# Cross attention: keys of two steps in one 512-column product

## The reference, cut to what matters

```python
q = (query @ Wq + bq).reshape(B, L, NKV, G, HDIM)        # 32 x 64 x 8 x 4 x 128
k_, v_ = jnp.split(kv @ Wkv + bkv, 2, axis=-1)           # 8 heads of keys and values
scores = jnp.einsum('blkgd,bmkd->bkglm', q, k) * scale   # 64 x 64 per batch and head
attn = jax.nn.softmax(scores, axis=-1)
o = jnp.einsum('bkglm,bmkd->blkgd', attn, v).reshape(B, L, NHEAD * HDIM)
return o @ Wo + bo
```

## Time and profile before

| | |
|---|---|
| median of three runs | 2743.34 us |
| profiled execution | 2743.87 us |
| its span | 2742.1 us |
| TensorE matmul busy | 2684.1 us, 98% |
| VectorE busy | 2022.1 us, 74% |
| GpSimd busy | 1621.1 us, 59% |
| ScalarE busy | 1537.9 us, 56% |
| granted clock of TensorE, mean | 0.994 |
| cross attention, first score matmul of step 0 | at 1642.16 us |

### The profile page before, as it was taken

How to read it: one execution, slowest core, us unless ns; L and a number is a source line. 1 busy time by engine, 2 the same in 40 slices (tenths; PEclk the granted TensorE clock), 3 DMA queues, 4 the chain that set the end, 5 groups by cost and what they waited for, 6 DMA issues and landing times.

```text
span 2742.1 us, 64050 instructions
## 1 busy us (share of the span) xinstructions
PE 2684.1 (98%) x26496; PEld 2374.8 (87%) x26496; DVE 2022.1 (74%) x4005; ACT 1537.9 (56%) x3207; POOL 1621.1 (59%) x1379
## 2 busy tenths in 40 slices
PE   7999999999999999999999999999999999999997
PEld 6889888889899999999998988888888888888876
DVE  6676667667677777667777668887778878777887
ACT  5566566656666665666665645554445455444445
POOL 6887887788777666676666763232324433333235
PEclk9999999999999999999999999999999999999998
DMA  6233223323325313322331331111112111111111
GB/s 177 77 93 99 86 80 103 94 70 104 107 61 168 92 48 88 84 72 72 84 87 52 83 98 43 35 54 39 45 41 59 51 43 40 50 35 43 32 32 62
DMA packets 91483, 197.70 MB, mean 72 GB/s; under 512 B 20664, under 2 KB 21304, under 8 KB 89144
## 3 DMA queue, kind: packets, MB, share of 16 engines
q1 hardware_dynamic: 71480, 154.80, 20.2%
q10 hardware_dynamic: 17664, 34.61, 3.8%
q0 software_dynamic: 2048, 4.20, 0.5%
HBM read 176.78 MB, written 16.78 MB: 71 GB/s over the span
## 4 chain that ended last, share of the span: by engine, by line
PE 84%; POOL 7%; DVE 5%; issue 2%; ACT 1%; DMA 0%; DVEq 0%; ACTq 0%
PE bank L1865 29%; PE big L1865 28%; PE bank L1957 14%; PE big L1937 12%; POOL ptl L799 3%; POOL gathered L774 2%; PE big L1957 2%; POOL wqTl L534 1%; ACT pth L981 0%; DVE xol L1514 0%; DVE P L1690 0%; POOL wkvTl L534 0%; PE big L1858 0%; POOL oTl L804 0%; DVE nmx L1417 0%
## 5 line engine op out<-in xcount | busy, mean ns | idle before, releaser
L799 POOL TENSOR_TENSOR ptl<-P,pth 128x576 fp32r<-128x576 f32 x512 | 727.5, 1438 | 291.1 <-ACT pth L981 290.6
L972 ACT ACTIVATE P<-big,nmx 128x576 f32<-128x576 f32 x512 | 378.4, 739 | 345.8 <-DVE nmx L1417 313.5
L1423 DVE STREAM_TRANSPOSE P<-P 128x576 f32<-128x576 f32 x512 | 395.2, 772 | 152.6 <-ACT P L972 147.2
L1957 PE MATMUL bank<-pth,v 32*128 32x256 f32 x4608 | 426.9, 282 | 11.0 <-POOL ptl L799 8.2
L1417 DVE TENSOR_REDUCE nmx<-big 128x1 f32<-128x576 f32 x512 | 384.8, 753 | 71.3 <-PE big L1937 58.2
L1957 PE MATMUL big<-pth,v 32*128 32x256 f32 x4608 | 427.4, 282 | 0.5 <-issue 0.4
L1957 PEld LDWEIGHTS bank<-pth,v 32*128 32x128 f32 x4608 | 364.6, 188 | 22.3 <-POOL ptl L799 11.9
L1957 PEld LDWEIGHTS big<-pth,v 32*128 32x128 f32 x4608 | 369.4, 188 | 1.0 <-issue 1.0
L981 ACT ACTIVATE pth<-P 128x576 fp32r<-128x576 f32 x512 | 340.6, 678 | 39.7 <-DVE P L1423 39.4
L880 POOL TENSOR_TENSOR P<-P,sm 128x512 f32<-128x512 f32 x64 | 67.3, 1051 | 487.3 <-DVE sm L1719 487.3
L1957 PE MATMUL big<-ptl,v 32*128 32x256 f32 x2304 | 336.4, 279 | 0.0
(11 more groups left out here) (283 smaller groups left out, 8008.5 us busy)
## 6 DMA issues: line engine op xcount, KB each, us to landing
rall<-kept_r ACTq DMA_DIRECT2D x64, 512.0 KB
raw<-in_wo SPq DMA_DIRECT2D x64, 256.0 KB
raw<-in_xWq SPq DMA_DIRECT2D x64, 256.0 KB
raw<-in_xWo SPq DMA_DIRECT2D x64, 256.0 KB
raw<-in_wq SPq DMA_DIRECT2D x62, 256.0 KB
v<-kept_v SPq DMA_DIRECT2D x24, 448.0 KB
v<-kept_v SPq DMA_DIRECT2D x68, 128.0 KB, 3.0
raw<-in_xWkv SPq DMA_DIRECT2D x32, 256.0 KB
```

The source lines that it names most:

```text
L799: pool.tensor_tensor(third_columns(ptl, i), blocks_of(i), f(third_columns(pth, i)), ALU.subtract).then_inc(p_low(i), 1)
L972: act.activation(P[:, i % PSLOTS, :].rearrange("p (k n) -> p k n", k=2), ps_s[i % 2][:, :, 0:HALF], ACT.Exp, bias=nmx[:, i % 8:i % 8 + 1], ...
L1423: dve.transpose(P[:, i % PSLOTS, :], P[:, i % PSLOTS, :]).then_inc(p_turned(i), 1)
L1957: m = pe.matmul(ps_o[a][:, 0:256], v[r, s, l, :], p[r, lo:hi + 1:hi - lo, block_of(b), :, :], start=first, stop=final)
```

## The change

For g + 1 >= 1, keys are made only in steps with odd s, for the 512 tokens of s - 1 and s together: 12 matmuls of 512 columns into one bank, one ScalarE instruction of 512 columns, two VectorE instructions of 256. `key_event` names the event that stands for both. Steps with even s make no keys. Those of g = 0 stay as they were. Waits on keys ask for the event of the pair; the order of bank requests follows.

```diff
--- before.py
+++ after.py
@@ -210,6 +210,11 @@
     if s == 2:
         return [("wq2", 4 * (g + 1) + j) for j in range(2, 4)] + ([("wk2", g + 2)] if g + 2 < GG else [])
     return [("wv2", g + 2), ("wv2", g + 3)] if g % 2 == 0 and g + 2 < GG else []
+
+
+def key_event(g, s):
+
+    return ("k", g, s | 1 if g else s)
 
 
 def late_block(g, s):
@@ -446,14 +451,20 @@
 
             return ap.rearrange("p (b q) o i -> p b (q o) i", q=2)
 
-        def key_high(s):
-            return by_parity(k2[:, 4 * s:4 * s + 4, :, :])[:, :, 0:4:3, :]
-
-        def key_low(s):
-            return by_parity(k2[:, 4 * s:4 * s + 4, :, :])[:, :, 1:3, :]
-
-        def key_columns(ps):
-            return ps[:, 0:256].rearrange("p (b q i) -> p b q i", q=2, i=64)
+        def key_tiles(g, s):
+            return pairs2(g, s - 1) + pairs2(g, s) if g else pairs2(g, s)
+
+        def key_rows_at(g, s):
+            return by_parity(k2[:, 4 * s - 4 if g else 4 * s:4 * s + 4, :, :])
+
+        def key_high(g, s):
+            return key_rows_at(g, s)[:, :, 0:4:3, :]
+
+        def key_low(g, s):
+            return key_rows_at(g, s)[:, :, 1:3, :]
+
+        def key_columns(ps, g):
+            return ps[:, 0:512 if g else 256].rearrange("p (b q i) -> p b q i", q=2, i=64)
 
         def weight_at(kind, n):
 
@@ -496,10 +507,10 @@
                 gate.wait_ge(q_done, (62 + n // 4, 1))
             elif kind == "ctx":
                 gate.wait_ge(kv_done, ("v", G - 2, n % HT // 2))
-                gate.wait_ge(kv_done, ("k", G - 1, n % HT // 2))
+                gate.wait_ge(kv_done, key_event(G - 1, n % HT // 2))
             elif kind == "fw":
                 gate.wait_ge(kv_done, ("v", GG - 2, n // 2))
-                gate.wait_ge(kv_done, ("k", GG - 1, n // 2))
+                gate.wait_ge(kv_done, key_event(GG - 1, n // 2))
             elif kind == "wq2" and n >= 4:
                 gate.wait_ge(q_done, (2, 2 * (n // 4) - 1, n % 4))
             elif kind == "wo2" and n >= 4:
@@ -510,7 +521,7 @@
                 gate.wait_ge(kv_done, ("v", n - n % 2 - 2, 3))
             elif kind == "fa":
                 gate.wait_ge(kv_done, ("v", GG - 2, 2))
-                gate.wait_ge(kv_done, ("k", GG - 1, 2))
+                gate.wait_ge(kv_done, key_event(GG - 1, 2))
             elif kind == "fb":
                 gate.wait_ge(kv_done, ("k", GG - 2, 3))
 
@@ -1036,7 +1047,7 @@
                 gate.wait_ge(kv_done, ("k", g, s))
                 if g >= 1:
                     gate.wait_ge(s_done, (2, 4 * (g - 1) + s, 1))
-                act.activation(key_high(s), key_columns(bank_at[("k", g, s)]), ACT.Identity,
+                act.activation(key_high(g, s), key_columns(bank_at[("k", g, s)], g), ACT.Identity,
                                bias=bqk[:, 32 + g % G:33 + g % G]).then_inc(kv_hi(("k", g, s)), 1)
 
             def value2_hi(g, s):
@@ -1237,7 +1248,7 @@
                         tile_high("x3", tt)
                     for a in work:
                         weight2(*a)
-                if g + 1 < GG:
+                if g + 1 < GG and s % 2 == 1:
                     key2_hi(g + 1, s)
                 if n in NORM_STEPS:
                     square_root(pairs2(G, NORM_STEPS.index(n)), 1)
@@ -1341,7 +1352,8 @@
                     put(("k", 0, 3))
                     put(("v", 0, 3))
                 if g + 1 < GG:
-                    put(("k", g + 1, s))
+                    if s % 2 == 1:
+                        put(("k", g + 1, s))
                     if g % 2 == 1:
                         put(("v", g + 1, s))
             for tt in range(HT, NT):
@@ -1496,8 +1508,8 @@
                 gate.wait_ge(kv_hi, ("k", g, s))
                 for par in range(2):
                     dve.scalar_tensor_tensor(
-                        key_low(s)[:, :, par, :], key_columns(bank_at[("k", g, s)])[:, :, par, :],
-                        bqk[:, 32 + g % G:33 + g % G], f(key_high(s)[:, :, par, :]), ALU.add, ALU.subtract).then_inc(
+                        key_low(g, s)[:, :, par, :], key_columns(bank_at[("k", g, s)], g)[:, :, par, :],
+                        bqk[:, 32 + g % G:33 + g % G], f(key_high(g, s)[:, :, par, :]), ALU.add, ALU.subtract).then_inc(
                             kv_lo(("k", g, s)), 1)
 
             def value2_lo(g, s):
@@ -2099,17 +2111,17 @@
                 products(ps, terms, q_done, (2, m, j))
 
             def key2(g, s):
-                c0 = 256 * s
+                c0, width = (256 * s - 256, 512) if g else (256 * s, 256)
                 wh, wl = wk_at(g)
                 ps = q_bank(("k", g, s), (kv_lo, ("k", g, s)))
                 wait_split(gate, "wk2" if g >= 1 else "xwk", g)
-                for t in pairs2(g, s):
+                for t in key_tiles(g, s):
                     wait_split(gate, "ctx", t)
                 terms = []
                 for c in range(NC):
                     w = slice(128 * c, 128 * c + 128)
-                    terms += split3(wh[:, w], wl[:, w], xTh[:, c, c0:c0 + 256], xTl[:, c, c0:c0 + 256])
-                products(ps[:, 0:256], terms, kv_done, ("k", g, s))
+                    terms += split3(wh[:, w], wl[:, w], xTh[:, c, c0:c0 + width], xTl[:, c, c0:c0 + width])
+                products(ps[:, 0:width], terms, kv_done, ("k", g, s))
 
             def value_rows2(g, s):
                 ps = q_bank(("v", g, s), (kv_lo, ("v", g, s)))
@@ -2128,7 +2140,7 @@
             def score2(n):
                 g, s = n // 4, n % 4
                 gate.wait_ge(q_lo, (2, n // 2, 3))
-                gate.wait_ge(kv_lo, ("k", g, s))
+                gate.wait_ge(kv_lo, key_event(g, s))
                 if n >= 1:
                     gate.wait_ge(sm_done, ("sum", n - 1, 1))
                 else:
@@ -2239,7 +2251,8 @@
                     key2(0, 3)
                     value_rows2(0, 3)
                 if g + 1 < GG:
-                    key2(g + 1, s)
+                    if s % 2 == 1:
+                        key2(g + 1, s)
                     if g % 2 == 1:
                         value_rows2(g + 1, s)
             values2(STEPS - 1)
```

## The result

The kernel after takes 2749.5 us (median of 18 runs, 2745.43 to 2753.77), the kernel before in the same session 2743.92 us (18 runs, 2740.74 to 2747.3): a ratio of 1.0021, 95% interval [1.0014, 1.0028]. So the change costs 5.6 us, clear of the noise but only 0.2%; 4.8 were forecast. Its profiled execution took 2746.2 us, with a span of 2744.4.

A forecast was written before the change was run, and what follows sets the result against it. TensorE, busy 98%, bounds the kernel, with a softmax chain beside it having 1.62 us of slack. -4.8 + 3.6 + 3.7 + 0.9 + 1.7 - 0.3 = +4.8 us gives 2748.1 us; 8-in-10 range 2744.5 to 2752.5.

The forecast's parts named there:

- wide matmuls, 30 pairs: Key matmuls on TensorE: 12 wide replace 24 narrow, -0.16 us per pair of steps, -4.8 us if TensorE never waits.
- s = 2 of even g, five: Steps 18, 26, 34, 50, 58: later softmax chain and query weight stall the next step 0.72 us each, +3.6 us.
- n = 10 and 42: Steps 10 and 42, layer-norm statistics between key conversion and chain: the pair of steps becomes 32.42 us; +3.7 us for both.
- n = 8 and 40: Steps 8 and 40, statistics behind the previous step's conversion: chain 14.43 us holds the values, +0.47 each, +0.9 us.
- the start: Steps 0 to 4: step 0's values still wait for the chain, so its saving is lost, and step 3 stalls; +1.7 us.
- g = 7: Value rows of step 29 come later, so their 0.16 us wait for VectorE to leave the bank goes; -0.3 us.
- rival C: Wide key matmul takes 0.240 us, saving nothing on TensorE; 2752.9 us, chance 0.03.
- Lengths: Step without keys 12.97 us, with wide keys 15.69 us; both 2.88 more with values.
- rival B: Wide key conversion, before the softmax addition, costs nearly what two cost, up to +1.08 us: 2754.7 us, chance 0.13.
- rival D: Chain adapts: part of its delay vanishes in VectorE's waits, 3.0 us less: 2745.1 us, chance 0.14.
- The rival that all is saved (A): TensorE keeps everything the wide matmuls save, without new stalls: 2738.2 us, chance 0.05.
- What should cost nothing: Steps 16, 24, 32, 48, 56 just fit by 0.13 us; s = 1 of even g fits with chain 15.3 us.

The follow-up runs named there:

- e5: Kernel after, but wide keys converted in halves: two ScalarE instructions of 256 columns and four VectorE ones of 128; 2754.68 us, ratio 1.0041 to the kernel before.
- e3: Kernel after, but both conversions of keys made in even-g steps moved later, inside the next step; 2745.96 us, ratio 1.0012 to the kernel before.
- e1: Kernel after, but wide keys only in the odd-g steps, which make value rows too; 2740.86 us, ratio 0.9997 to the kernel before.
- e2: Kernel after, but wide keys only in the even-g steps, which make no value rows; 2750.39 us, ratio 1.0027 to the kernel before.
- e4: Kernel after, but in s = 2 both query weights split ahead of the softmax weights, in g = 7 before the bias additions; 2772.7 us, ratio 1.0109.
- e9: Kernel after with layer-norm work moved to long steps, even-g key conversions later, bias additions last, only the first query weight ahead; 2734.34 us, ratio 0.9972.
- e11: Same reordered kernel as e9, but wide keys in odd-g steps only; 2735.69 us, ratio 0.9979 to the kernel before.
- e7: Kernel after with key conversions later, both query weights ahead and layer-norm work in long steps; 2744.05 us, ratio 1.0003 to the kernel before.
- e8: Kernel before, narrow keys, with the same three edits as e7; 2742.07 us, ratio 0.9995 to the kernel before.

## Why the prediction was right, point by point

The stretch of 60 steps parts the +5.45 us by groups of four steps (after minus before; a group without a stall has -0.32):

| term of the sum | predicted | measured | from |
|---|---|---|---|
| wide matmuls, 30 pairs | -4.8 | -4.8 | groups g = 1, 3, 5, 9, 11, 13 at -0.32 to -0.34 |
| s = 2 of even g, five | +3.6 | +3.3 | steps 19, 27, 35, 51, 59: 16.32 to 16.36, less 15.69 |
| n = 10 and 42 | +3.7 | +3.9 | pair 10/11 32.47, pair 42/43 32.46 |
| n = 8 and 40 | +0.9 | +1.1 | steps 9 and 41: 16.22 and 16.21, less 15.69 |
| the start | +1.7 | +1.6 | group g = 0, +1.31 |
| g = 7 | -0.3 | +0.4 | group g = 7, +0.12 |
| sum | +4.8 | +5.5 | the stretch: +5.45 |

- **Wide matmul, rival C.** 2.72 us for twelve, as taken from the 512-column products of the earlier trace rows. C is refuted. The saving per matmul removed was 2 x 120 - 226.7 = 13.3 ns. The Trainium skill ("TensorE: Matmul & The Clock Gate", section "Back-to-back issue gap") has 2.5 ns for it, in its formula for an isolated warm matmul; this stream of fp32r matmuls doesn't agree, and the measurement decides.
- **Lengths.** Steps of 12.97 to 12.98 and 15.69 us; forecast 12.97 and 15.69.
- **Conversion, rival B.** Forecast +0.22 on ScalarE and +0.20 on VectorE; measured 0.69 - 0.47 = 0.22 and 0.88 - 0.61 = 0.27. The addition came 0.40 later and the chain 0.38, for 0.42. e5 is the price of B, and after doesn't have it.
- **The stall behind s = 2.** 0.65 us on the mean for 0.72, from the two places named; e3 parts it into 0.4 of conversion and 0.25 of query weight. Nothing in the chain gave (rival D): e3 and e5 moved the chain by -0.40 and +0.39, and the whole of each shows in the step.
- **The rival that all is saved (A)** is refuted by the 10.1 us of new waits, and its place shown by e1, where there is room, against e2, where there isn't.
- **What should cost nothing, cost nothing:** steps 16, 24, 32, 48 and 56 have chains of 13.81 to 13.83 us and no stall behind them, and steps 17 and 25 fit with chains of 15.49 and 15.24 (15.3 forecast).
- **The miss: g = 7.** The step "they come 1.28 us later in the long step, and the wait goes" was right for step 29, which is 19.48 us, 0.41 less than 18.61 + 1.28. But step 31 takes 20.51 us, 1.02 more than the 18.21 + 1.28 it should. The prediction looked at g = 7 for the value rows alone and not at GpSimd. Its timeline after, end of step 30, with TensorE below:

```profile
2131.34 1.30 POOL L894 TENSOR_TENSOR xpl<-P,xph 128x512 fp32r<-128x512 f32 x1 [1.49 <-ACT xph L1245]
2132.60 2.54 POOL L866 TENSOR_TENSOR xaccb<-xaccb,bob 128x512 f32<-128x512 f32 x2
2135.11 2.51 POOL L545 TENSOR_TENSOR wqTl<-raw,wqTh 128x512 fp32r<-128x512 f32 x2
...
2136.52 0.47 PE L1877 MATMUL bank<-yTh,wqTh 128*128 128x512 f32 x1 [0.98 <-POOL wqTl L545]
```

Two additions of the bias, 2.54 us, stand between the softmax weights and the query weight. Without them the weight would be there before TensorE; with them it is the release. Before, step 30 was 1.6 us longer and covered them. e4 and e9 put the additions last, and step 31 fell to 19.48: the cause is shown. It is the same mechanism as in the steps s = 2, overlooked in one place.

The forecast of the time, 2748.1, is 1.4 us below the measured median. 0.6 of that is its base: it started from 2743.34, the median of three runs, where the 18 runs of before have 2743.92. 0.65 is the sum above. The 0.1 left is far inside the interval of the ratio, which is 3.8 us wide.

The work behind the stretch can't be told apart at this size. From the first scores of step 60 to those of step 63 the profiles have 45.24 us before and 45.84 after, other kernels of this case 42.3 to 45.9. The granted clock in step 62 is 0.90 in before and after and 1.00 in e9 and e11, which have 42.3 and 42.7.

The sum had no term for the clock. That step 11 of after kept its full clock, where e2, e3, e4 and e5 lost 1.0 to 1.6 us in it, was not foreseen: to that extent the closeness of the number is luck.

## What to carry to other kernels

Where one engine is full and a dependency chain runs beside it, a saving on the full engine is worth no more than the chain's slack in the steps that get shorter; list for each step its length, the chain's length, and what stands directly behind the chain's last instruction, before work is joined in a way that makes steps uneven (here 1.44 of 1.62 us of slack were given away, and eleven late starts turned -4.8 us into +5.5). Find the slack first and save then: with the statistics, the conversion, one weight and the bias additions moved, the wide keys brought 3.8 to 4.6 us of stretch. An idle stretch of GpSimd isn't free for the asking: here work in it cost nothing beside VectorE's reduction, and 1.0 to 1.1 us beside an instruction with two operands in SBUF.

## What the runs showed that was not expected

**VectorE held by GpSimd** until GpSimd's instruction is over (e4, e7 and e8, above).

**The clock of TensorE** fell to its lower level, 1.2 GHz, in eleven steps of four profiles: step 11 of e2 and of e3, steps 11 and 43 of e5, and seven steps of e4. In e3 TensorE had waited 1.79 us for the softmax weights and then 0.36 for the query weight. Timeline of TensorE in e3 behind that wait:

```profile
1812.84 0.39 PE L1881 MATMUL bank<-yTl,wqTh 128*128 128x512 f32 x1
1813.06 0.56 PE L1881 MATMUL bank<-yTh,wqTl 128*128 128x512 f32 x1
1813.42 0.63 PE L1881 MATMUL bank<-yTh,wqTh 128*128 128x512 f32 x1
1813.85 0.63 PE L1881 MATMUL bank<-yTl,wqTh 128*128 128x512 f32 x1
```

From start to start 0.22 us, then 0.36 and 0.43. Busy time by stretch of e3 (length, then TensorE busy, and behind it the granted clock, DMA share and GB/s):

```profile
1811.00:1814.00 3.00, 2.45 (x17) 0.86 0.20 61
1814.00:1817.00 3.00, 3.00 (x10) 0.58 0.62 191
1817.00:1820.00 3.00, 3.00 (x15) 1.00 0.03 10
```

Ten matmuls in 3 us at a granted clock of 0.58, fifteen at 1.00. Step 11 took 19.57 us, its twin, step 43, 17.96 in the same execution with no fall: 1.6 us. After's profile waits 2.13 us in the same place and shows no fall in its steps 10 and 11; in e4, step 51 fell behind a wait of 2.28 us, and step 59 did not behind one of 2.27. So a wait of some 2 us in an otherwise full stretch cost either nothing or 1.0 to 1.6 us; what decides between them stays open here. All of it is from one profile each.
